# A three-layer decoder kernel: the norm of a tile pair and the row stores moved inside the expert stage's software pipeline

## The reference, cut to what matters

```
for e in range(n_experts):
    mask = (max_ind == e)[:, None]
    y = gelu(x @ W1[e], approximate=False) @ W2[e]      # 128 -> 512 -> 128
    out = out + mask * y
out = out * max_prob
x = _layernorm(x + out)                                  # (v - mean) / sqrt(var + 1e-5)
```

## Time and profile before

| | |
|---|---|
| median of 3 runs | 1726.66 us (1726.17 to 1730.73) |
| the profiled execution's own time | 1726.34 us |
| span of its profile | 1724.3 us |
| first transpose of the expert stage | at 1552.02 us |
| last matmul ends | at 1700.83 us |
| last indirect DMA issued | 1715.26 to 1716.23 us |
| PE, DVE, ACT, POOL busy, share of the span | 86%, 75%, 63%, 70% |

### The profile page before, as it was taken

The page is one execution under the profiler, slowest core; times in us unless marked ns, Lnnn a source line. Parts: engine busy times, 40 slices in busy tenths (PEclk is TensorE's granted clock), DMA queues, the critical chain, the costliest instruction groups (busy, mean ns, idle before and its releaser), DMA issues. The chain is left out here.

```text
span 1724.3 us, 21744 instructions
## 1 busy us (share of the span) xinstructions
PE 1490.1 (86%) x6178; PEld 887.3 (51%) x6178; DVE 1290.3 (75%) x2194; ACT 1080.9 (63%) x2151; POOL 1199.8 (70%) x863
## 2 busy tenths in 40 slices
PE   4888899888998889988885899999999999819994
PEld 1333334333433334333332577777777777619994
DVE  1999999999999999999992356566666666624542
ACT  3767777777777777777763566565666665404553
POOL 1799999999999999999994114446446445443665
PEclk8889999999999999999988999899999999959997
DMA  3445454454554445444441802113023000017771
GB/s 129 149 148 173 147 165 161 158 166 145 165 168 155 155 147 178 160 170 148 148 134 26 333 5 104 56 69 115 17 104 120 13 1 14 12 30 212 211 206 50
DMA packets 105848, 214.19 MB, mean 124 GB/s; under 512 B 12162, under 2 KB 56709, under 8 KB 105744
## 3 DMA queue, kind: packets, MB, share of 16 engines
q1 hardware_dynamic: 101200, 204.50, 36.9%
q0 software_dynamic: 4544, 8.47, 1.4%
HBM read 168.28 MB, written 45.56 MB: 124 GB/s over the span
## 5 line engine op out<-in xcount | busy, mean ns | idle before, releaser
L321 POOL TENSOR_TENSOR hc<-state,c_rows 128x1024 f32<-128x1024 f32 x256 | 599.0, 2360 | 42.3 <-DVE state L503 33.9
L606 PE MATMUL ps_y<-hc,ident 128*128 128x512 f32 x1024 | 515.0, 646 | 91.3 <-POOL hc L321 91.3
L503 DVE TENSOR_TENSOR_SCAN state<-ps_da,inp 128x512 f32<-128x512 f32 x512 | 591.6, 1205 | 0.0
L395 ACT ACTIVATE ps_da<-dt,a_neg 128x512 f32<-128x512 f32 x512 | 349.1, 688 | 172.0 <-DVE state L503 167.9
L606 PEld LDWEIGHTS ps_y<-hc,ident 128*128 128x128 f32 x1024 | 202.4, 203 | 382.1 <-issue 232.1
L492 DVE TENSOR_TENSOR inp<-dtx,ps_b 128x1024 f32<-128x1024 f32 x192 | 231.8, 1207 | 35.3 <-ACT ps_b L401 19.2
L918 POOL TENSOR_TENSOR rs<-ms,m_half 128x4 f32<-128x4 f32 x48 | 49.5, 1032 | 243.9 <-DVE ms L1144 243.8
L308 POOL TENSOR_TENSOR inp<-dtx,b_rows 128x1024 f32<-128x1024 f32 x64 | 150.9, 2358 | 0.1
L552 PE MATMUL ps_misc<-x1T,w_conv 128*128 128x512 f32 (+3 forms) x256 | 119.3, 611 | 23.7 <-ACT x1T L346 15.3
L401 ACT COPY ps_b<-b_rows 128x512 f32<-128x512 f32 x192 | 111.6, 581 | 26.3 <-DVE inp L492 24.5
L1056 ACT ACTIVATE ex<-sc,nmx 77x128 f32<-77x128 f32 x192 | 74.7, 390 | 74.0 <-DVE nmx L1153 74.0
(11 more groups left out here) (210 smaller groups left out, 2735.3 us busy)
## 6 DMA issues: line engine op xcount, KB each, us to landing
b_rows<-bc_rows SPq DMA_DIRECT2D x128, 512.0 KB, 4.9
c_rows<-bc_rows SPq DMA_DIRECT2D x128, 512.0 KB, 4.0
sorted_x<-pad_rows SPq DMA_DIRECT2D x8, 4160.0 KB, 13.4
w<-in_L_ffn_W SPq DMA_DIRECT2D x78, 256.0 KB
xrow<-sorted_x SPq DMA_DIRECT2D x39, 130.0 KB, 2.4
x_tok<-in_x SPq DMA_DIRECT2D x16, 256.0 KB, 4.5
ctx<-in_ctx SPq DMA_DIRECT2D x16, 154.0 KB
out_x<-orow,target POOLq DMA_INDIRECT x78
```

Source lines behind the costliest of these rows:

```text
L321: pool.tensor_tensor(hc[:, n % RING], state[:, n % RING], over_c(c_rows[:, slot, n % 2]), ALU.mult).then_inc(hc_ready, 1)
L395: act.activation(ps_da[u % DA_RING][:], dt[:, par, c], ACT.Exp, scale=a_neg[:, c, n:n + 1]).then_inc(da_ready, 1)
L503: dve.tensor_tensor_scan(state[:, n % RING, c], ps_da[u % DA_RING][:], inp[:, n % RING, c], 0.0, ALU.mult, ALU.add).then_inc(state_ready, 1)
L606: ins = pe.matmul(ps_y[:, c], ident[:], hc[:, n % RING, c], start=False, stop=n == NS - 1)
```

## The change

The DVE takes `shift` of a pair in the turn of its `variances`, right behind them, no longer a turn later behind `column`. ACT takes `normalised` of both tiles of a pair in the even turn, four and three tiles behind, and none in the odd one. POOL stores a tile five turns behind and no longer six; in the turns below 39 (`tail` is false) the store stands ahead of `root`, in those from 39 on behind it. POOL's loop is one turn shorter. No instruction is added or removed.

```diff
@@ POOL
         def tile(j, buf, turn, half):
-            if buf % 2 == 0 and within(j, 4):
+            tail = isinstance(j, int) and j >= NJ
+            paired = buf % 2 == 0 and within(j, 4)
+            if paired and tail:
                 root(j - 4, earlier(buf, turn, 4)[0], half - 2)
-            if within(j, 6):
-                store(j - 6, earlier(buf, turn, 6)[0])
-        over_tiles(pool, tile, 6)
+            if within(j, 5):
+                store(j - 5, earlier(buf, turn, 5)[0])
+            if paired and not tail:
+                root(j - 4, earlier(buf, turn, 4)[0], half - 2)
+        over_tiles(pool, tile, 5)
@@ ACT
-            if within(j, 5):
-                last, last_turn = earlier(buf, turn, 5)
-                normalised(j - 5, last, last_turn, half - 2)
+            if buf % 2 == 0:
+                for back in (4, 3):
+                    if within(j, back):
+                        normalised(j - back, *earlier(buf, turn, back), half - 2)
@@ DVE
-            if buf % 2 and within(j, 5):
-                shift(j - 5, earlier(buf, turn, 5)[0], half - 2)
             if within(j, 3):
                 last, last_turn = earlier(buf, turn, 3)
                 gated(j - 3, last, last_turn)
                 moments(j - 3, last)
             if buf % 2 == 0 and within(j, 4):
                 variances(j - 4, earlier(buf, turn, 4)[0], half - 2)
+                shift(j - 4, earlier(buf, turn, 4)[0], half - 2)
```

## The result

The changed kernel took 1740.73 us in the median of five runs (1740.07 to 1742.32), against 1726.66 for the kernel before (five runs on the same chip, 1724.13 to 1730.73). The ratio is 1.0077, 95% interval 1.0061 to 1.0093: slower by 14 us, outside the forecast range. The same file measured twice more gave 1733.61 (ratio 1.0049, 1.0031 to 1.0067) and 1745.5 (ratio 1.0099, 1.0068 to 1.013). An occasion is one batch of executions on one chip, with one of them profiled. The traces of the three occasions show this one program with two loops. I call them the loop on time (8.0 us a pair) and the late loop (8.6 us a pair).

What follows compares the result with a forecast made beforehand. PE was taken to pace the loop at 7.46 us a pair, POOL the end. A new 7.86 us POOL loop costs 8.8 us, the end gives back 4.4: 1730.7 us against 1726.34, range 1724 to 1734.

Steps and rivals of the forecast that it cites:

- The ring: Expert-stage loop: root, shift, norm, four DMAs, next root; claimed 7.86 us a pair against PE's 7.46.
- four DMAs: POOL's stores of one pair, between norm and next root: three spacings of 1.28 and a last 0.97, 4.81 us.
- the shorter tail: End of the expert stage from root(34): five tiles left to store, not six; gives back 4.4 us.
- The signs foretold: Loop trace: PE waits for column some 0.4 us a pair, DVE waits on POOL at L1647, POOL otherwise has 0.3 gaps.
- the register term: Norm's waits in the hardware loop, with semaphore values computed in registers: 0.02 us a pair taken, bounds 0 and 0.1.
- The term trusted least: Norm to first DMA on POOL: the 0.86 us after the activations keeps its size when the wait follows a root.
- The start: First pairs of the expert stage, up to the first PE stall: root(4) at 1585.53, column 11 0.3 us late.
- shift start to norm start 0.20: Step from the DVE's shift to ACT's norm in the closed loop, claimed to take 0.20 us.
- a Gelu 0.1 late: ACT in the loop: norms end 0.1 us after the next tile's first Gelu is due, claimed to cost nothing.
- Rival 1: Waits overlap and PE still paces the loop, the 0.86 falling to about 0.4: 1723.4 us, chance 0.13.
- Rival 2: POOL's store DMAs themselves grow beside other DVE work, up to 0.09 us each, 5.4 us on top: 1736.1 us, chance 0.07.
- Rival 3: Stall in the loop and gain in the tail cancel within 1 us: 1726.5 us, chance 0.12.

Runs made afterwards that it cites:

- e1: Changed kernel with root ahead of the store in every turn, not only the last ones: 1722.38 us, ratio 0.9976.
- e2: Changed kernel with one indirect DMA a tile in place of two, so half of the output rows are not stored: 1714.67 us, ratio 0.9931.
- e6: Changed kernel without the shift; the norm waits for root itself and adds the mean instead: 1729.45 us, ratio 1.0019.
- e11: Changed kernel with shift put back in the odd turn, behind column: 1733.47 us, ratio 1.004.
- e17: Changed kernel, unedited, measured a second time: 1733.61 us, ratio 1.0049.
- e18: Changed kernel, unedited, measured a third time: 1745.5 us, ratio 1.0099.
- e3: Kernel before, with POOL storing two tiles in each even turn, four indirect DMAs in one run: 1728.71 us, ratio 1.001.
- e15: Kernel before, with stores in runs of four DMAs and the loads of two tiles issued together: 1729.77 us, ratio 1.0019.

## Why the prediction was right or wrong

**The ring was right.** The prediction said that root, shift, norm, four DMAs and root form a closed loop that is longer than PE's 7.46, that shift ahead of column passes it to PE, and that the shorter tail gives a part back. e1 opens the loop and e2 shortens it below PE's pace, and both times the loss is gone. e6 cuts the link to the DVE, and PE is full again; e11 shows that the place ahead of column isn't the only way to PE, since behind it `gated` passes the delay on. The signs foretold are there in e17: the DVE waits for POOL at shift, PE waits for column in ten recorded places, 0.45 us each (about 0.4 forecast), and POOL has gaps of 0.3 and one wait a pair.

**The loop's terms were a little small.** Forecast 7.86 us a pair, measured in the loop on time 7.98 (root(4) at 1593.26 to root(34) at 1712.93 in e17, 15 pairs). Step by step in e17:

| step | forecast | measured |
|---|---|---|
| root to shift | 1.08 | 1.09 to 1.10 |
| shift to norm | 0.20 (+0.02) | 0.20; 0.29 in one pair of three |
| norm to first DMA | 1.73 | 1.76 |
| four DMAs | 4.81 | 4.90 (1.34 + 1.28 + 1.30 + 0.98) |
| last DMA to root | 0.02 | 0 |

The largest error is the first spacing. The prediction used 1.28 three times in the loop, and in the tail "1.04 + 0.30" for a first DMA. The DMA behind a root takes 1.04 in the earlier trace rows already, and in the new order every pair's first DMA is such a one: the row was read and applied in one place only. With 0.03 from norm to DMA, and the register term at 0.03 in the mean where 0.02 was taken, the terms give the 0.12 a pair, 1.8 us over 15 pairs. The term trusted least, the 0.86 behind a root, is off by 0.03 alone.

**The start was 0.4 us late.** Root(4) came 33.20 us after the first column in e17 (1593.26 - 1560.06), forecast 32.78 (1585.53 - 1552.75), by the same terms in the two rings ahead of it. So PE lost its first time one pair early, at column 9 and not 11. With 0.1 us more of tail the sum is 1.8 + 0.4 + 0.1 = 2.3; the stage grew by 6.8 where 4.4 was forecast. For executions with this loop, 1731 to 1734 us, the forecast's 1730.7 is short by about that, and the range of 1724 to 1734 holds them.

**The step that failed** is "shift start to norm start 0.20". In the late loop it is 0.75 to 0.91 us (0.86 in the pair shown), since the norm is not held by shift but by the Gelus ahead of it in ACT's queue. The prediction had these as done by then: it let the Gelus of tile 6 end 25.85 us after the first column (1578.60 - 1552.75), and in the first profile they held norm(2) until 27.2 (1578.24 - 1551.04). It took it as given that a Gelu starts when its matmuls are done, and priced the one delay of ACT that it saw, a Gelu 0.1 late, at "nothing". In the first occasion and in e18 the Gelu started up to 2.9 us after that in even turns. The late loop is 9.4 us of stage (187.7 - 178.3): 0.65 ahead of root(4) and 8.7 in the 15 pairs from there to root(34), while the tail is the same 17.3. The measurement of 1740.73 us has this loop, and the forecast is 10 us below it. That part of the loss had no place in the prediction at all, neither in the sum nor in a rival.

**What makes the signals late stays open.** What the traces show is the tie to POOL: the Gelus start 0.89 to 1.03 us after its run of four DMAs ends, while their distance from their own matmuls moves by 0.5 us. That points at the run of DMAs, or at something that goes with it, as what holds up ACT's and SP's queues; it isn't shown. A run of four isn't enough by itself, for e17, e3 and e15 have it and are on time. But e3 and e15 were measured once each, as were the kernels without weight loads, and an occasion that would have been on time anyway tells nothing of the cause. All three traces with late Gelus (the first, e18, and in part e11) have the closed ring; eight others have it without them, one of the same program. The edited rings were on time in all seven measurements (e11 aside), the unedited one in one of three: that may be the edits, the chip or chance, and these runs can't tell. Chip 4 by itself doesn't decide, as it had both. Nor is it shown that an occasion keeps to one loop: only one execution of each was traced, and the two untraced executions of e17 at 1740.27 and 1740.36 us fit the late loop as well as the loss ahead of the stage.

**Rival 1 is out.** The 0.86 between the norm's second activation and the DMA keeps its size in the ring, where the wait follows a root: 1.76 from norm to DMA in e17, 1.75 in the late loop. POOL is busy for 32.08 of 50 us in e17 and still sets PE's pace. The Trainium skill (Perfetto Trace Analysis, Identifying the Most-Contended Engine) ranks engines by occupancy, but judges TensorE by MFU (the share of its peak rate that the matmuls reach) and by the busy share of its weight loads. By the second of these PE, with weight loads busy for 44.14 of 50 us in e17, stands ahead of POOL in the very stretch in which POOL's ring holds it back, so here the measurement decides against the ranking.

**Rival 2 holds a small part.** The median DMA grew from 968 ns to 979, in the first profile and in e17, and to 978 in e1:

```profile
L1566 POOL DMA_INDIRECT out_x<-orow,target x78: 977/979/1057, 1580.4 to 1729.3; - x78
```

Over four DMAs and 15 pairs this is 0.7 us, a part of the 1.8 above, and not the 5.4 of its bound. (The prediction let it decide from 0.01 us a DMA; 60 x 0.01 on top of 4.4 is 5.0, so it takes 0.014 to pass 5.2.) e3, built on the kernel before, stays at 969. The longest stays at 1057, so nothing of the size of a DVE instruction was added to any of them; a lock of the shared port, of which the Trainium skill (SBUF — State Buffer, Who interferes with whom) speaks, doesn't show as a delay of these issues.

**Rival 3 is out** too: stall and tail don't cancel in either loop.

## What to carry to other kernels

When an instruction moves on one queue, follow the ring that it closes through the other engines, with the gaps between issues and the waits in it, and compare its length with the bound's pace; busy shares don't show it. Put a small operation that other engines wait for ahead of its queue's own long work: root ahead of the stores turned +0.5 to +1% into -0.24%. And before you explain a difference of under 1%, measure the same file on another occasion: four edits looked like a cure here until the unedited kernel showed the same times. When a start is late, compare its distance to every engine, and not only to the one that it waits for in the code.

## What the runs showed of the hardware

- One program showed two loops, 7.97 and 8.6 us a pair. The occasions with the slower one in their trace ran 1740.07 to 1742.32 and 1738.25 to 1749.94 us, the other mostly 1731.22 to 1733.86. In the slower one ACT's Gelus start up to 3.9 us behind their first matmul and not 1.07, always 0.89 to 1.03 us after the end of POOL's run of four indirect DMAs (30 of 30 waits), and SP's register instructions take 3 to 666 ns and not 37. The granted clock in the stretch is 1.00 in both.
- An indirect DMA on POOL follows the one ahead of it after 1.28 us, but after 1.34 when that one is the first behind a root; it is busy for 0.98 or 1.04. Behind ACT's last activation it waits for 0.86 to 0.9 even when POOL is idle.
- In the hardware loop, with semaphore values computed in registers, a norm starts 0.20 us behind the shift in two pairs and 0.29 in the third (e17).
